# Storing the residual output tile by tile, and loading an expert slot's slips one slot later

## What is computed

```
x = x + _L0_xattn_ref(_layernorm(x, axis=-1), ctx_1024, ...)     # 16 batches x 64 queries x 1601 keys
x = x + _L0_attn_ref(_layernorm(x, axis=-1), L0_attn_Wq, ...)    # gives x, the residual output of this text
x = x + _L0_ffn_ref(_layernorm(x, axis=-1), L0_ffn_w1, ...)      # top 2 of 8 experts per token
# ffn: combine = (one_hot(sel) * topk_w).sum(axis=1)
#      h = einsum('td,eid->tei', x, w1); y = h[..., INTER:] * silu(h[..., :INTER])
#      out = einsum('tei,ehi,te->th', y, w2, combine)
```

## Time and profile before

| | us |
|---|---|
| median of 3 runs | 2503.81 (2503.28 to 2506.72) |
| the profiled execution | 2511.19 |
| its span in the trace | 2509.4 |
| TensorE busy in it | 2368.8 (94%) |

### The profile page before, as it was taken

One profiled execution on the slowest core, in us unless ns is written; L12 is line 12 of the kernel. 1 busy time (PEld: TensorE's weight loads), 2 busy tenths in 40 slices (PEclk: granted clock), 3 DMA queues, 4 the chain that ended last, 5 costly groups with the idle time before them and its releaser, 6 DMA issues. The chain is left out here.

```text
span 2509.4 us, 41288 instructions
## 1 busy us (share of the span) xinstructions
PE 2368.8 (94%) x14585; PEld 2090.4 (83%) x14585; DVE 1276.0 (51%) x2146; ACT 1092.3 (44%) x1866; POOL 1117.5 (45%) x470
## 2 busy tenths in 40 slices
PE   8999999999999999999999999999659966999997
PEld 6798998889899888989988898998527745999986
DVE  3255555555455555555555554555655454555542
ACT  3354544445454444445444454544512213444442
POOL 2255555555555555555555555555520023142323
PEclk9999999999999999999999999999879987999999
DMA  4311121221112122111212211121040027455544
GB/s 153 106 41 47 43 62 38 66 56 41 48 44 61 34 70 55 41 48 45 60 34 70 56 41 48 45 60 31 3 159 1 11 80 192 141 151 163 162 143 84
DMA packets 147889, 177.59 MB, mean 71 GB/s; under 512 B 83152, under 2 KB 106576, under 8 KB 147664
## 3 DMA queue, kind: packets, MB, share of 16 engines
q1 hardware_dynamic: 137952, 147.63, 19.9%
q10 hardware_dynamic: 4608, 16.78, 2.2%
q0 software_dynamic: 5104, 10.24, 2.2%
HBM read 135.12 MB, written 39.48 MB: 70 GB/s over the span
## 5 line engine op out<-in xcount | busy, mean ns | idle before, releaser
L394 POOL TENSOR_TENSOR k_parts<-k_t,k_parts 64x1602 fp32r<-64x1602 f32 x128 | 426.4, 3331 | 450.0 <-DVE k_parts L459 449.9
L715 PE MATMUL ps_kv<-ctx_hi,wk_hi 128*128 128x256 f32 (+1 forms) x1536 | 463.5, 302 | 7.8 <-DVE ctx_lo L573 7.4
L715 PE MATMUL ps_kv<-ctx_lo,wk_hi 128*128 128x256 f32 (+1 forms) x1536 | 441.2, 287 | 0.0
L715 PE MATMUL ps_kv<-ctx_hi,wk_lo 128*128 128x256 f32 (+1 forms) x1536 | 441.0, 287 | 0.0
L505 DVE TENSOR_TENSOR probs_t<-ps_pt,probs_t 128x512 fp32r<-128x512 f32 x368 | 205.9, 559 | 447.3 <-ACT probs_t L624 445.0
L408 POOL TENSOR_TENSOR v_parts<-v,v_parts 128x832 fp32r<-128x832 f32 x128 | 283.2, 2212 | 335.5 <-ACT v_parts L642 333.9
L715 PE MATMUL ps_kv<-wv_hi,ctx_hi 128*128 128x512 f32 (+1 forms) x832 | 340.7, 409 | 1.8 <-DVE wv_lo L543 1.8
L715 PE MATMUL ps_kv<-wv_hi,ctx_lo 128*128 128x512 f32 (+1 forms) x832 | 327.6, 394 | 0.0
L715 PE MATMUL ps_kv<-wv_lo,ctx_hi 128*128 128x512 f32 (+1 forms) x832 | 326.7, 393 | 0.0
L612 ACT ACTIVATE k_t<-ps_kv,bk_sb 128x256 f32<-128x256 f32 (+1 forms) x384 | 186.1, 485 | 313.2 <-PE ps_kv L715 307.8
L715 PEld LDWEIGHTS ps_kv<-ctx_hi,wk_hi 128*128 128x128 f32 x1536 | 292.2, 190 | 10.9 <-issue 8.6
(11 more groups left out here) (257 smaller groups left out, 4128.9 us busy)
## 6 DMA issues: line engine op xcount, KB each, us to landing
ctx_raw<-ctx_dram SPq DMA_DIRECT2D x81, 512.0 KB, 3.8
w_raw<-w_dram SPq DMA_DIRECT2D x64, 512.0 KB, 4.2
rows_in<-zeros SPq DMA_DIRECT2D x150, 128.0 KB, 3.6
w_raw<-w_dram ACTq DMA_DIRECT2D x32, 512.0 KB
ctx_raw<-ctx_dram SPq DMA_DIRECT2D x16, 644.0 KB, 5.5
q_blocks<-q_parts SPq DMA_DIRECT2D x256, 32.0 KB, 1.9
rows<-rows_in SPq DMA_DIRECT2D x8, 768.0 KB
q_parts<-probs_t SPq DMA_DIRECT2D x16, 256.0 KB, 2.0
```

Of the source, the lines that this page charges most:

```text
L394: nc.gpsimd.tensor_tensor(k_parts[64 - 64 * s:128 - 64 * s, :], k_t[par][64 * s:64 * s + 64, g, :], k_parts[64 * s:64 * s + 64, :].bitcast ...
L715: last = nc.tensor.matmul(o, still, moving, start=(k == 0 and i == 0), stop=(k == DT - 1 and i == 2))
```

## The change

The two stores of `x2` leave slot 0. SyncE, which before waited for all eight tiles before the slots, now waits for each tile's `x_added` in turn and stores that tile: eight stores of 256 KB to `out`, and for the first four tiles a second one of 256 KB to the spare rows. `load_slips(s)` leaves unit 6 of slot s, and is now issued in unit 5 of slot s + 1; the last slot's follows after all slots. The waits inside it are the same, with one on `tables_done` added for slot 0 (the table that it reads was waited for before by `load_rows(1)` anyway).

```
+X_STORES = 16 * (TT + SPARE // P)
...
                 if is_first(s):
                     sp.wait_ge(slips_stored, 16 * 2 * TT)
+                    sp.wait_ge(tables_done, 5)
...
-                    if u == RAW and is_first(s):
-
-                        ov = out[0:NT, :].rearrange("(t p) d -> p t d", p=P)
-                        sp.dma_start(ov, x2[:]).then_inc(x_stored, 16)
-                        sp.dma_start(out[NT:, :].rearrange("(t p) d -> p t d", p=P), x2[:, 0:SPARE // P, :]).then_inc(x_stored, 16)
-                    if u == IT - 2:
-                        load_slips(s, par)
+                    if u == IT // 2 + 1 and not is_first(s):
+                        load_slips(s - 1, 1 - par)
...
-            sp.wait_ge(x_added, TT)
-            over_slots(sp, slot)
-            sp.wait_ge(x_stored, 32)
+            for t in range(TT):
+
+                sp.wait_ge(x_added, t + 1)
+                sp.dma_start(out[t * P:(t + 1) * P, :], x2[:, t, :]).then_inc(x_stored, 16)
+                if t < SPARE // P:
+                    sp.dma_start(out[NT + t * P:NT + (t + 1) * P, :], x2[:, t, :]).then_inc(x_stored, 16)
+            load_slips(over_slots(sp, slot), 1)
+            sp.wait_ge(x_stored, X_STORES)
...
                 if is_first(s):
-                    pool.wait_ge(x_stored, 32)
+                    pool.wait_ge(x_stored, X_STORES)
```

## The result

| | us |
|---|---|
| before, median of 4 runs | 2505.26 (2503.28 to 2506.74) |
| after, median of 4 runs | 2491.62 (2488.82 to 2493.16) |
| ratio | 0.9943, 95% interval 0.9928 to 0.9958 |
| profiled execution after, and its span | 2492.94, 2491.2 |

The change takes 13.6 us off the median. The prediction was 2482.9 with a range of 2479 to 2495: the sign and the range hold, the size doesn't. 20.9 us were expected. The time lies outside the forecast's own case (2480 to 2488, given 74%) and inside that of the rival "supply" (2488 to 2498, given 14%); the range holds only because it took in most of that rival. Between the two traces the difference of the spans is 18.2 us (2509.4 to 2491.2).

What follows compares the result with a forecast made beforehand. One w1 load behind 3 MB of stores was taken to stall slot 0. Gains of 16.7 + 2.7 + 0.6 + 0.9 = 20.9 us took 2511.19 to 2490.3, and 7.4 less for the median gave 2482.9 us, range 2479 to 2495.

Steps and rivals of the forecast that it cites:

- forecast's own case: Whole kernel: the summed gains hold and the time falls at 2480 to 2488 us; 74%.
- supply: Slot 0: weight loads meeting the slips scatters stop ScalarE at the w2 split; gain only about 10 us, 2493.8; 14%.
- What bounds the kernel: Slot 0: w1 piece 4, queued behind 3 MB of stores, stalls ScalarE 15.95 us and TensorE 15.23 us.
- The stores leave slot 0: Slot 0: w1 piece 4 comes in time, ScalarE's 15.95 us wait goes, TensorE's unit 4 starts earlier; 16.7 us gained.
- so unit 4 starts at 2096.7: Slot 0: y(2) is ready in time, so TensorE starts unit 4 at 2096.7 us instead of 2113.35.
- The clock: Slot 0: without the stall TensorE keeps 2.4 GHz; 2.7 us in unit 4, 0.6 in unit 6 (bounds 0 and 1.2).
- The wait for the slips: Slot 0: SyncE's 23.3 us wait for slips scatters stood beside ScalarE's stall; moving it alone gains nothing, 0 us.
- The stores in the tile loop: Tile loop: twelve 256 KB stores fit into the pauses between adds and delay nobody; price 0 us.
- The slips of later slots: Later slots: w1 pieces 6 and 7 come earlier, which helps only in slot 6; 0.9 us.
- the median lies 7.4 lower: Whole kernel: the median was taken as 7.4 us under the profiled execution, turning 2490.3 into 2482.9 us.
- The stall wasn't the stores': Slot 0: slips scatters alone hold the engines, piece 4 still lands near 2107 us, 0.9 us remain, 2502.9; 4%.
- collision in later slots: Slots 2 to 7: earlier w1 loads collide with accumulating stores, up to 7.3 us a slot; slower, 2527 us; 4%.

Runs made afterwards that it cites:

- e3: Changed kernel with the two whole stores back in slot 0, only the slips' loads moved: 2505.14 us, ratio 0.9999 to the kernel before.
- e9: Kernel with only the slips' loads moved, whole stores in slot 0, and slips scatters issued after the second w2 piece: 2494.18 us, ratio 0.9955.
- e4: Changed kernel with GpSimd's sixteen slips scatters issued behind its second w2 piece of slot 0: 2487.81 us, ratio 0.9929 to the kernel before.
- e2: Changed kernel with slips loaded in unit 6 of their own slot as before, so only the stores moved: 2500.95 us, ratio 0.9977.
- e1: The changed kernel run again, unaltered: 2493.87 us, ratio 0.9958 to the kernel before.
- e5: Changed kernel with w2 pieces 0 and 1 of slot 0 issued by ScalarE before the slots: 2492.84 us, ratio 0.994.
- e8: Changed kernel with two whole stores of 2 MB and 1 MB after the last tile's add, replacing the twelve small ones: 2495.94 us, ratio 0.9945.
- e12: Changed kernel with early w2 pieces, four scatters behind each w2 piece of slot 0, and slot 1's turned rows rounded first: 2485.13 us, ratio 0.992.
- e7: Changed kernel with w1 pieces 5 and 6 of slot 0 held back until piece 3 is split: 2497.73 us, ratio 0.995.
- e6: Changed kernel with both late slips scatters and early w2 pieces 0 and 1 in slot 0: 2489.29 us, ratio 0.9925.

## Why the prediction was right or wrong

*What bounds the kernel.* Right on the place: one late w1 piece in slot 0, and slots 1 to 5 shift as they are (the gain is 16.55 us from slot 1 to slot 6). Wrong on the cause, in one half. The prediction read "the DMA engines were full" as the work of 3 MB of stores. It had the sign of the other half before it: 215 GB/s at a share of 1.04 against 310 at 0.89. It put the difference down to the stores, and gave scatters as the whole cause 4% as a rival; e3 and e9 show that the rate was the scatters'. By the Trainium skill's rule on queues ("DMA: Bandwidth & Descriptors", section Queues, rings and completion order) the prediction called supply less likely, since the w2 piece never stood behind the stores. That was no help: in after the piece on ScalarE's queue, with no store ahead on any queue, took 9.58 us.

*The stores leave slot 0, 16.7 us.* The 15.95 us of wait at piece 4 are gone, as said. The step that was too large is "so unit 4 starts at 2096.7". From the first matmul that is 19.36 us; it came at 21.44. Ahead of y(2) the working took the w2 split with no wait, though the row gave only that the piece was there by 2108.77; the wait is 4.75 us. And its list of what stands ahead left out VectorE's low part y_lo, which is 2.50 us in the chain of after. Alone y_lo would have cost nothing: in e4 it took 2.55 us in the same place and TensorE had no gap. **2.1 us too much.**

*The clock, 2.7 + 0.6.* Unit 4 ran at the full clock, as said, and unit 6 too (the 12.51 us for three units in the chain are 4.17 each, so the whole 1.2 came, not half). But the clock fell in the wait of 2.40 us behind unit 4: 0.58 in 2104 to 2108, unit 5 took 5.13 us instead of 4.19, its turned rows 1.11. From unit 4's start to unit 6's end the kernel before took 21.80 us, the forecast's terms leave 18.5, and after took 19.80. **1.3 us too much.** The late w2 piece is behind this as well: ScalarE and VectorE were still catching up, and the first wait for turned rows grew from 1.78 to 2.40 us. These two make 3.4 of the 3.45 us that slot 0 fell short (20.0 expected, 16.55 measured).

*The wait for the slips, 0.* Right alone (e3), and no harm in slot 1: the loads at 2116 wait for nothing. But "this edit alone would gain nothing" is half of the story. Without it 5.3 us are gained (e2) and not 12.4 (e1). The sum hides that, since it took the edit together with the stores.

*The stores in the tile loop, 0.* Right. From the first to the last add the loop takes 71.8 us in the traces of before, e1, e4 and e5 and 74.1 to 74.3 in those of after, e2, e3 and e8, of which e3 and e8 have no store in the loop. The two values come with and without the stores, so they aren't the stores'. The twelve land in 2.1 us in the median. Views of after: the DMA issues from 1970 to 2060 us (KB, us to landing) and the adds:

```profile
out_dram<-x SPq DMA_DIRECT2D x12, 256.0 KB, 2.1
```

```profile
L1577 DVE TENSOR_TENSOR x<-ps_one,x x8: 691/692/692, 1972.8 to 2047.1; 128x512 f32<-128x512 f32 x8
```

The rule of 1 MiB per DMA in the Trainium skill ("DMA: Bandwidth & Descriptors", section Bandwidth), weighed in the prediction, cost nothing here, as the rows had it: e8 with large pieces isn't faster (0.9945).

*The slips of later slots, 0.9.* 0.44 came, at slot 6, and 0.99 in e1's trace.

*From the trace to the median.* This is the largest part of the miss. The terms missed by 2.65 us in the trace: 3.45 in slot 0 and 0.46 in slot 6 too much, less the 1.24 by which slot 0 began earlier, up to rounding. The other 6.1 us come of one sentence: "the median lies 7.4 lower". The prediction carried the 7.4 us by which the profiled execution of before was over its median to the kernel after. There the profiled execution is only 1.3 us over (2492.94 to 2491.62). Some 1.5 of the 7.4 were a median of three runs that rose from 2503.81 to 2505.26 with the fourth. And in e1 to e12 the profiled execution lies between 4.1 us under and 4.5 over its kernel's median, so such a distance changes from one kernel's trace to the next. Of the 30 runs of before that came with e1 to e4 and e9 to e12 (2503.46 to 2511.18) only one is as long as the profiled 2511.19, which is 5 us above their medians. Of these 5 us, 1.2 lie ahead of slot 0: its first matmul is at 2077.34, and at 2076.10 in the median of the 13 other traces. Where the rest lies isn't known. If it lay in the very stall that the change removes, the median gain had to be smaller than the trace's; no run shows that. The late silu(1) of before, below, isn't the place, since ScalarE waited for piece 4 behind it in any case.

*The rivals.* Supply, at 14% and 2493.8, had the nearest time and the right sign in the trace: ScalarE stopped at the w2 split. Its price was too high (unit 4 at 2106; it was 2097.5), and the amount of weights that it went by wasn't the cause (e7). "The stall wasn't the stores'" was the other half of the truth. Nothing of a collision in later slots shows: slots 1 to 5 are as long as before and slot 6 is shorter. So the right range is partly luck: the time was moved to there by a late w2 piece that the sum didn't have, and by a distance from the median that didn't carry over.

## What to carry to other kernels

A busy share of the DMA engines near 1 must be read with the bytes beside it: where the rate is well under what the same loads reach elsewhere in the trace, look for small transfers in flight, and move these first. A wait that is covered today is worth what it costs once the cover is gone, so edit and cover have to be tried together. And when the profiled execution is well off the median, that distance isn't a constant to be carried over; it may be chance or lie in the stall itself, and belongs in the range.

## What the runs showed of the hardware

- Sixteen scatters of 128 x 8 bytes, 16 KB in all, go with a fall of what the DMA engines move beside 3 MB of stores from 392 to 398 GB/s to 224 to 275 at the same busy share. With no stores beside it, a 512 KB load takes 9.58 us with them in flight (after) and 5.1 without (e4). The loss comes and goes: with scatters in flight 351 GB/s were reached as well (after, 2078 to 2084). And it isn't bound to their packets: in e7, from 2104 to 2106 us, with a single scatter packet left, the engines moved 92 GB/s at a share of 0.91.
- While scatters are in flight, ScalarE and TensorE now and then stand still for 1 to 10 us with nothing in the profile that releases them. From silu(0) to silu(1) of slot 0 it is 4.16 or 4.17 us in all six traces in which no scatter is in flight by then (e4, e6, e9 to e12). Of the eight with early scatters only after and e5 have 4.16; e8 has 4.69, e3 5.86, e1 6.80, before 7.85, e2 10.11 and e7 12.89, with waits marked "remote" (7.25 us in e2, above) or gaps of 1.0 to 1.1 us between matmuls marked "issue". What these engines wait for stays open. The profile lists instruction loads as DMAs of their own queue, and in nine traces one of 16 KB moves in the first half of slot 0: in before at 2091.0 to 2091.5, where silu(1) starts at 2091.38, but in e3 at 2089.5 to 2090, behind silu(1) at 2088.13. So late instruction loads are not shown to be the cause.
- VectorE's y_lo (128x384, two inputs) takes 0.55 us alone and 2.5 when GpSimd's w_lo, of 2.4 us, has just begun: in after GpSimd's runs from 2094.13 to 2096.51 and y_lo from 2094.43 to 2096.93. The Trainium skill ("SBUF — State Buffer", section Who interferes with whom) says that GpSimd and a VectorE instruction with two inputs from that memory share a port when the GpSimd instruction reads it too, as w_lo does, and that the second waits for the whole of the first. These times agree: y_lo ends 0.42 us after GpSimd's in both after and e4.
- One chip ran the kernel before some 3.5 us slower (2509.81) than the two others (2506.24, 2506.27).
